# TensorE's order in the attention stage of a fused attention and mixture-of-experts kernel: groups of three crossed pairs, then one or two value tiles

## The reference

```python
xn = _layernorm(x, axis=-1)
Q = (xn @ Wq.T).reshape(H, b, s, dkh)        # H = 16, dkh = 16; K and V alike
scores = jnp.einsum('hbqd,hbkd->hbqk', Q, K)
atten = jax.nn.softmax(scores, axis=-1)
out = jnp.einsum('hbqk,hbkd->hbqd', atten, V).reshape(b, s, -1)
y = out + xn
att = (y - mean(y, (1, 2))) / sqrt(var(y, (1, 2)) + EPS)
ffn = sum over the two chosen experts of gate * ((xn @ w_in[e].T) @ w_out[e].T)
x + att + ffn
```

## Time and profile before

| | us |
|---|---|
| runs of the kernel before | 1051.34, 1048.86, 1052.19 (median 1051.34) |
| the profiled execution: its own time | 1055.4 |
| the profiled execution: its span | 1053.6 |
| TensorE matmuls busy | 1012.4 (96%) |
| TensorE weight loads busy | 527.1 (50%) |
| VectorE busy | 873.8 (83%) |
| ScalarE busy | 627.3 (60%) |
| GpSimd busy | 78.7 (7%) |
| mean granted TensorE clock | 0.981 of full |

### The profile page before, as it was taken

One profiled execution on the slowest core, in us unless ns is written; L12 is line 12 of the kernel. 1 busy time (PEld: TensorE's weight loads), 2 busy tenths in 40 slices (PEclk: granted clock), 3 DMA queues, 4 the chain that ended last, 5 costly groups with the idle time before them and its releaser, 6 DMA issues.

```text
span 1053.6 us, 20712 instructions
## 1 busy us (share of the span) xinstructions
PE 1012.4 (96%) x7816; PEld 527.1 (50%) x7816; DVE 873.8 (83%) x1255; ACT 627.3 (60%) x1231; POOL 78.7 (7%) x205
## 2 busy tenths in 40 slices
PE   6778999999999999999999999999999999999995
PEld 6666888888886533333333333333333333333332
DVE  4301777877877989999999999999999999999976
ACT  2100111111110178888888888888888888888885
POOL 2100111011100001000100010001000100010001
PEclk9899999999999989999999999999999999999998
DMA  7777456445555012222222222222222222222214
GB/s 274 271 246 223 130 161 181 129 133 158 144 162 160 5 52 62 71 61 70 62 70 62 69 61 69 62 70 61 70 62 71 60 70 61 71 60 71 63 25 160
DMA packets 127042, 108.58 MB, mean 103 GB/s; under 512 B 81120, under 2 KB 102368, under 8 KB 126944
## 3 DMA queue, kind: packets, MB, share of 16 engines
q1 hardware_dynamic: 114016, 86.03, 29.6%
q10 hardware_dynamic: 12928, 21.24, 5.9%
HBM read 80.75 MB, written 42.21 MB: 117 GB/s over the span
## 4 chain that ended last, share of the span: by engine, by line
PE 89%; DVE 5%; DMA 4%; issue 1%; SPq 0%; ACT 0%; ACTq 0%; POOL 0%; POOLq 0%; DVEq 0%
PE ps L892 27%; PE ps L874 22%; PE ps L829 15%; PE ps L862 11%; PE ps L801 5%; PE ps L775 3%; DMA wp<-w_out_t 3%; PE ps L790 2%; PE ps L903 2%; DVE negm L620 1%; PE ps L915 1%; DVE acc L608 1%; PE ps L763 1%; DVE xnc L733 0%; DMA qf<-ot 0%
## 5 line engine op out<-in xcount | busy, mean ns | idle before, releaser
L620 DVE TENSOR_REDUCE negm<-ps 128x1 f32<-128x1024 f32 x512 | 618.5, 1222 | 31.9 <-PE ps L862 15.3
L464 ACT ACTIVATE wp<-ps 128x512 f32<-128x512 f32 x684 | 369.4, 602 | 88.7 <-PE ps L874 62.6
L874 PE MATMUL ps<-qf,kf 50*128 50x512 f32 x1024 | 388.1, 455 | 2.1 <-DVE ps L679 1.7
L862 PE MATMUL ps<-kf,qf 48*128 48x512 f32 x1024 | 368.1, 451 | 0.2 <-DVE negm L620 0.2
L874 PEld LDWEIGHTS ps<-qf,kf 50*128 50x128 f32 x1024 | 160.5, 186 | 207.4 <-ACT wp L464 107.7
L892 PE MATMUL ps<-wp,vb 128*17 128x256 f32 x2736 | 215.7, 387 | 0.3 <-issue 0.3
L862 PEld LDWEIGHTS ps<-kf,qf 48*128 48x128 f32 x1024 | 146.3, 186 | 7.5 <-issue 5.7
L464 ACT ACTIVATE vstage<-ps 128x512 f32<-128x512 f32 x170 | 102.3, 602 | 24.6 <-PE ps L874 11.2
L829 PE MATMUL ps<-mth,xth 128*128 128x512 f32 x256 | 103.8, 405 | 3.4 <-DVE spare L552 2.4
L892 PEld LDWEIGHTS ps<-wp,vb 128*17 128x17 f32 x2736 | 46.9, 95 | 118.5 <-ACT picks L464 42.8
L464 ACT ACTIVATE picks<-ps 128x512 f32<-128x512 f32 x170 | 102.4, 602 | 0.0
(11 more groups left out here) (104 smaller groups left out, 675.9 us busy)
## 6 DMA issues: line engine op xcount, KB each, us to landing
feat_d<-qk_d SPq DMA_DIRECT2D x64, 256.0 KB, 4.5
qf<-feat_d SPq DMA_DIRECT2D x128, 128.0 KB
wp<-w_in SPq DMA_DIRECT2D x16, 512.0 KB, 4.3
wp<-w_out_t SPq DMA_DIRECT2D x16, 512.0 KB, 5.2
qk_d<-stage ACTq DMA_DIRECT2D x32, 256.0 KB
qk_d<-spare ACTq DMA_DIRECT2D x32, 256.0 KB
qf<-feat_d SPq DMA_DIRECT2D x128, 64.0 KB
kf<-feat_d SPq DMA_DIRECT2D x128, 64.0 KB
```

What stands on the lines that cost most here:

```text
L464: nc.scalar.activation(weight_tile(n, j, b)[:, h * HALF:(h + 1) * HALF], ps[:, ST_BANK[(2 * unit + b) % 3], :], ACT.Exp).then_inc(exp_done, 1)
L620: nc.vector.tensor_reduce(negm[:, n % 2, qt:qt + 1], ps[:, b:b + 2, :].rearrange("p b c -> p (b c)"), AX.X, ALU.max, negate=True).then_inc ...
L862: last = nc.tensor.matmul(ps[:, MAX_BANK[turn % 2] + half, :], qf[rows, u, qt * P:(qt + 1) * P], kf[rows, u, :], start=True, stop=True)
L874: nc.tensor.matmul(ps[:, ST_BANK[(2 * unit + half) % 3], :], kf[rows, u, j * P:(j + 1) * P], qf[rows, u, h * HALF:(h + 1) * HALF], start=T ...
```

## The change

TensorE's loop over (n, j, h) becomes a loop over half-steps k = 16 n + s. After each half-step with k mod 3 = 2 a group ends (PHASE = 3), and only there do transposes and value tiles come; value tile number t (counted through all batches) is issued at the first group end with k >= 2 t + 9, at most up to the end of a batch's tiles. `crossed_scores` now issues one half-step: a score and one half of a maximum. The places in VectorE's and ScalarE's lists (the first rows, the normalisation, `pv_out`) and in the numbering of turns follow.

```diff
--- before.py
+++ after.py
@@ -41,6 +41,8 @@
     TPB = NT // BATCH
     EARLY = BATCH - 1
     LAG = 2
+    PHASE = 3
+    HALVES = 2 * NKT
 
     x_v = x.rearrange("a (t p) d -> p (a t) d", p=P)
     out_v = out.rearrange("a (t p) d -> p (a t) d", p=P)
@@ -200,6 +202,20 @@
         o_done = sem("o_done")
         o_out = sem("o_out", 4)
 
+        def phase_end(n, s):
+
+            return (HALVES * n + s) % PHASE == PHASE - 1
+
+        def border(n):
+
+            return next(s for s in range(4 * LAG - 1, HALVES) if phase_end(n, s))
+
+        def rows_at(n):
+
+            return next(s for s in range(4 * LAG + 3, HALVES, 2) if phase_end(n, s))
+
+        first_rows_at = next(s for s in range(5, HALVES, 2) if phase_end(0, s))
+
         max_turn, row_turn, first_turn = {}, {}, {}
 
         def next_turn():
@@ -214,9 +230,9 @@
             for qt in range(NKT):
                 if n + 2 < NB:
                     max_turn[n + 2, qt] = next_turn()
-                if n == 0 and qt == 2:
+                if n == 0 and qt == first_rows_at // 2:
                     first_turn[1] = next_turn()
-                if qt == 2 * LAG + 1 and n % 2 == 0 and n > 0:
+                if qt == rows_at(n) // 2 and n % 2 == 0 and n > 0:
                     row_turn[n // 2 - 1] = next_turn()
         row_turn[NB // 2 - 1] = next_turn()
 
@@ -480,7 +496,7 @@
                 for j in range(NKT // 2):
                     for h, b in ((0, 0), (0, 1), (1, 0), (1, 1)):
                         exps(n, j, h, b)
-                        if (j, h, b) == (LAG - 1, 1, 0) and n:
+                        if 4 * j + 2 * h + b == border(n) and n:
                             pv_out(n - 1)
             pv_out(NB - 1)
 
@@ -683,9 +699,9 @@
             for n in range(NB - 2):
                 for qt in range(NKT):
                     maxima(n + 2, qt)
-                    if n == 0 and qt == 2:
+                    if n == 0 and qt == first_rows_at // 2:
                         first_rows(1)
-                    if qt == 2 * LAG + 1 and n % 2 == 0 and n:
+                    if qt == rows_at(n) // 2 and n % 2 == 0 and n:
                         normalise(n // 2 - 1)
                     if n % 2 == 1 and n > 1 and qt == 1:
                         statistics((n - 1) // 2 - 1)
@@ -852,6 +868,8 @@
                 if turn >= 2:
                     pe.wait_ge(turn_done, turn - 1)
 
+            means_at = [next(s for s in range(first, HALVES) if phase_end(NB - 2, s)) for first in (4, 12)]
+
             def max_scores(n, qt, halves=(0, 1)):
                 u, turn = n % SLOTS, max_turn[n, qt]
                 if qt == 0:
@@ -875,12 +893,13 @@
                                  qf[rows, u, h * HALF:(h + 1) * HALF], start=True, stop=True
                                  ).then_inc(st_ready[half], 1)
 
-            def crossed_scores(n, j, h):
-                scores(n, j, h, 0)
+            def crossed_scores(n, j, h, half):
+                if half == 0:
+                    scores(n, j, h, 0)
                 if n + 2 < NB:
-                    max_scores(n + 2, 2 * j + h, (1,))
-                    max_scores(n + 2, 2 * j + h, (0,))
-                scores(n, j, h, 1)
+                    max_scores(n + 2, 2 * j + h, (1 - half,))
+                if half == 1:
+                    scores(n, j, h, 1)
 
             def sum_values(n, j, b):
                 if j == 0 and b == 0:
@@ -937,25 +956,28 @@
                 pe.wait_ge(ff_added[j], 2 * NT)
             pe.wait_ge(att_const, 3)
 
-            for n in range(NB):
-                for j in range(NKT // 2):
-                    for h in range(2):
-                        crossed_scores(n, j, h)
-                        if n == 0 and j == 1 and h == 0:
-                            maxima_to_rows(1)
-                        if j == LAG and h == 1 and n % 2 == 0 and n:
-                            to_token_rows(n // 2 - 1)
-                        if n == NB - 2 and j in (1, 3) and h == 0:
-                            mean_over_partitions(0, slice(0, EARLY), j // 2)
-                        if j >= LAG:
-                            sum_values(n, j - LAG, h)
-                        elif n:
-                            sum_values(n - 1, NKT // 2 + j - LAG, h)
-                        if n and j == LAG - 1 and h == 1 and n + 1 < NB:
-                            maxima_to_rows(n + 1)
-            for j in range(NKT // 2 - LAG, NKT // 2):
-                for b in range(2):
-                    sum_values(NB - 1, j, b)
+            summed = 0
+            for k in range(HALVES * NB):
+                n, s = divmod(k, HALVES)
+                crossed_scores(n, s // 4, s // 2 % 2, s % 2)
+                if not phase_end(n, s):
+                    continue
+                if n == 0 and s == first_rows_at:
+                    maxima_to_rows(1)
+                if n % 2 == 0 and n and s == rows_at(n):
+                    to_token_rows(n // 2 - 1)
+                if n == NB - 2 and s in means_at:
+                    mean_over_partitions(0, slice(0, EARLY), means_at.index(s))
+                while 2 * summed + 4 * LAG + 1 <= k:
+                    m, tile = divmod(summed, NKT)
+                    sum_values(m, tile // 2, tile % 2)
+                    summed += 1
+                    if tile == NKT - 1:
+                        if m + 2 < NB:
+                            maxima_to_rows(m + 2)
+                        break
+            for tile in range(summed - NKT * (NB - 1), NKT):
+                sum_values(NB - 1, tile // 2, tile % 2)
             to_token_rows(NB // 2 - 1)
 
             for which in range(2):
```

## The result

The changed kernel takes 1104.23 us (median of 4 runs, 1101.89 to 1105.44), the kernel before 1051.76 on the same chip: a ratio of 1.0485, interval 1.0446 to 1.0523. The forecast was 1100, range 1064 to 1124.

The account below looks back on a forecast made before the run. TensorE's order was taken to bound the kernel at 1.22 us a step. Per six batches, loop 63.2 plus extras 5.1 made 68.3 us; overall +49 on 1055.4 gave 1104, on the median's footing 1100 us, range 1064 to 1124.

Parts of the forecast that it names:

- The loop: Closed loop through the split turn and two VectorE reductions: three turns can't take less than 3.95 us, against 3.66 before.
- The one unseen price: On TensorE, from the late, lone maximum to its value tile: taken as 0.44 us, between 0.32 and 0.56.
- TensorE's own sum: TensorE alone: 1.46 us for a group with one value tile, 1.89 with two, 3.35 per three turns.
- the output transposes: Ahead of the value tiles they wait for turn 1's reduction: 0.95 us every second batch, 2.85 per six batches.
- B: Group ending on an odd half-step: second half of turn 1, both of turn 2, then two value tiles.
- the DMA of the maxima's rows: TensorE's wait before a batch's first score: 0.5 to 0.86 us, booked as 0.7 per six batches after slack.
- the slack: TensorE's spare 0.5 us in the loop, between the end of B and the point where turn 2's reduction lets it go on.
- signs of being wrong: Reductions 1.14 us apart without gaps, a lone maximum finding its bank free, or granted clock below 1 after 390 us.
- 0.78 us of extras: Kernel before, per batch beyond its steps: maxima's transpose 0.21 us, output transposes every second batch, a wait for the maxima's DMA.
- Rival 1: The split turn costs nothing; VectorE bounds at 3.42 us per three turns: about 1011 us; chance 0.09.
- A's third pair: Last pair of a group ending on an even half-step, holding turn 1's first half; comes 0.57 us after the first pair.
- Rival 4: TensorE's waits drop the clock to 1.2 GHz, 5.8 us each time; five falls make 1129 us; chance 0.07.

Follow-up runs that it names:

- x1: Changed kernel with VectorE's maxima taken over one bank of two and an exponential scale of 0.25: 1036.90 us, ratio 0.9836.
- x2: Kernel before with VectorE's maxima taken over one bank of two and an exponential scale of 0.25: 1048.78 us, ratio 0.9958.
- y2: Changed kernel with value tiles dealt the other way, two after the split turn's first half, one after the whole turns: 1210.53 us, ratio 1.1511.
- x3: Changed kernel with groups of two pairs instead of three, the moved transposes and output copy kept: 1046.73 us, ratio 0.9953.
- x4: Changed kernel with groups of three scores kept but maximum matmuls regrouped so that no turn is split: 1089.95 us, ratio 1.0338.
- y1: Changed kernel with the output transposes behind the group's value tiles instead of ahead of them: 1085.97 us, ratio 1.0324.
- z1: Kernel before with ScalarE's copy of a batch's output one exponential later: 1047.16 us, ratio 0.9965.
- z2: Changed kernel with groups of four pairs, two whole turns and then two value tiles: 1092.72 us, ratio 1.0395.

## Why the prediction was right

**The loop.** Its seven terms were 0.05, 0.44, 0.56, 0.50, 0.04, 1.14 and 1.23; the timeline has 0.05, 0.42, 0.56, 0.53 for the next two together, 1.14 and 1.22. The one unseen price, from the lone maximum to its value tile, is 0.42, near the 0.44 taken between 0.32 and 0.56. x1 and x2 show that the loop goes through the reductions, y2 that what stands between the halves of a turn is paid in full, x3 that nothing is lost once the grouping is undone. x3 doesn't single out the split, since it takes away the groups of three as well; x4 shows that such groups meet another loop without it.

**TensorE's own sum.** 1.46 us for a group with one tile was right, and x1 shows it as soon as VectorE no longer holds it.

**The batch.** The row of the maxima's transpose, which answers to the earlier trace rows:

```profile
L934 PE MATMUL ps<-ident,mpart x53: 276/277/278, 401.9 to 993.9; 128*16 128x128 f32 x53
```

(993.9 - 401.9)/52 = 11.38 us, forecast 11.39. Such agreement is partly luck, since two terms missed in opposite directions. One is the output transposes. From the late maximum half ahead of them to the next one, over the first pair of B, the transposes' weight load and their idle time:

```profile
618.11 0.18 PEld L880 LDWEIGHTS ps<-kf,qf 48*128 48x128 f32 x1 [0.32 <-DVE negm L636]
619.10 0.50 PE L892 MATMUL ps<-qf,kf 50*128 50x512 f32 x1
620.98 0.42 PEld L922 LDWEIGHTS ps<-ident,ot 128*128 128x128 f32 x4 [1.35 <-issue]
623.15 0.18 PEld L880 LDWEIGHTS ps<-kf,qf 48*128 48x128 f32 x1
```

The transposes start 1.88 us after B's first pair (1.89 in the sum), but the whole way takes 623.15 - 618.11 = 5.04 us. The three such places of six batches take 5.1, 5.2 and 5.4, the last with a second value tile of 0.43 in it: some 3.5 us above three loops of 3.93, where 3 x 0.95 = 2.85 was booked. y1 shows that only 18 of the 26 us booked for moving them can be had. The other term is the DMA of the maxima's rows, booked with 0.7 per six batches beyond the slack. It is the releaser in 12 places for 5.8 us in all, most of that the 0.42 of layout: it costs nearly nothing. The 9.0 us that I read in the kernel before as a wait for this DMA were mostly layout too.

**What the sum didn't have.** Behind the stage's start the clock fell three times, for 3.4 us each, every time at an output transpose: at 437.3, 710.4 and 983.4 us. The stretch ahead of the first fall, and one around it:

```profile
433.80:437.20 3.40, 2.45 (x19) 0.89 (x16) 2.75 (x4) 3.12 (x7) 0.00 (x0) 1.00 0.18 61
436.00:439.50 3.50, 2.57 (x20) 1.22 (x20) 2.94 (x4) 1.51 (x3) 0.32 (x1) 0.68 0.15 37
```

From one late maximum half to the next, the first of them took 6.77 us (434.18 to 440.95); the next place of the same kind, at the full clock, took 5.22 (503.64 to 508.86). The other two falls took as long: 1.55 us each, 4.6 together. That is the distance from 1100 to the measured 1104, if one wants to name it, but the two mis-sized terms are as large. One of the prediction's own signs of being wrong (a granted clock below 1 after 390 us) was thus seen, at a small price. In the kernel before, the copy ahead of an exponential costs 4 us (z1); these stood unnamed in its 0.78 us of extras. And the step of 1.2 us read in the earlier trace rows from 1022.80 to 1024.00 holds a transpose of the maxima (0.21, at 1023.79), so a step there is nearer 1.0; nothing was booked on it.

**The rivals.** Rival 1 needed the slot free at A's third pair. It was free 0.48 us after it where the loop was tight, over 0.35 in 77 of 141 groups, and in time in 33. Its rule from the Trainium skill, TensorEngine Tiling (Array Packing), Key Properties, that a change of tiling mode drains TensorE, agrees with these traces (0.36 and 0.42 us idle at each turn of layout). Fewer changes do pay, but little: of the 12 us between x1 and x2 some 4 to 6 may be the moved copy's, while 0.31 us per three turns over 61 batches would be 50 us. x1's extras, 8.3 us per six batches against 4.7 in the kernel before, take most of that back. They pay only where nothing else holds TensorE. Rival 4 took place in y2 and hardly here.

## What to carry to other kernels

When an in-order engine's work is regrouped, look at the buffers whose fill and drain the new order stretches: write down the closed loop (slot freed, refill's first part, what now stands inside the refill, its last part, the consumer, slot freed) and compare its sum with each engine's own. An engine that is busy 96% and that almost nothing waits for can be the largest term of the next loop. And a wait is worth what it adds to the idle time that stands there anyway, not the number in its row.

## What the runs showed of the hardware

- TensorE's weight load starts 0.05 us after the end of the reduction that it waits for, in the changed kernel as in the earlier trace rows, wherever the reduction is what it waits for.
- The granted clock fell from 1.00 to the lower level behind a stretch with TensorE busy for 2.45 of 3.4 us, although the longest wait ahead of an output transpose is 1.3 us. In y2_two_after_a, where TensorE was busy 92 to 94 in 100 us, the mean clock was 0.91 to 0.96 in the rows shown. TensorE: Matmul & The Clock Gate in the Trainium skill (Why this matters for your kernels) warns of idle gaps between bursts; here it fell with many small waits and no long gap. In y1, without the longest of them, it stayed at 1.00 from 400 to 1000 us.
- The exponentials' banks and the maxima's banks each set a limit of this kernel on the length of a group: the fourth score came 1.19 us after the first (z2), and a maximum half that waited came 0.05 us after the end of the reduction two turns back. With three score banks and two pairs for maxima, groups of two pairs were the longest that paid here.
